# A vision tower's feed-forward on tokens sorted by expert, and softplus split into Exp, Ln and a clip

## The chip, the cores and the metric

The kernel runs on one core of one Trainium2 chip. Five engines work in parallel, each with its own queue of instructions: PE (TensorE, matmuls and transpositions), DVE (VectorE), ACT (ScalarE, functions from tables), POOL (GpSimd) and SP, which here only issues DMAs. They wait for each other by semaphores. The metric is the device time of one launch in microseconds; a run's time is a little longer than the span that the profile shows.

## The reference

All in float32. x is (4, 512, 256, 4), the stream h is 4 batches of 512 tokens of width 256.

```python
h = einsum('bhid,oi,od->bho', x, weighted_sum, weight)
h = h + attn(layernorm(h))        # 4 layers, the same weights in each:
    # x = rmsnorm(x) ; xr = x @ W_in ; x_in, res = split(xr)
    # u = silu(conv4(x_in) + conv_b) ; dbl = u @ W_x  -> dt, B, C
    # delta = softplus(dt @ W_dt + b_dt)
    # h_t = exp(delta_t * A) * h_(t-1) + delta_t * u_t * B_t   (16 states, 512 channels)
    # y = sum_state(h_t * C_t) + u * Dp ; x = (y * silu(res)) @ W_out
h = h + ffn(layernorm(h)):
    # z = layernorm(h)
    # e = argmax(z @ W_router)                  (4 experts, one for each token)
    # t = gelu(z @ W1[e] + b1[e])               (256 -> 1024)
    # out = layernorm(t @ Wo + bo + z) * gamma + beta
```

## The kernel before, in words

The program has three parts. It begins with the token product and its norm. Then comes the scan stage: 16 steps k, one batch of one layer each (k = layer * 4 + batch). A step walks over 16 states s and, in each, over four quarters d of the 512 channels; one pair (s, d) is a slot. In a slot TensorE transposes delta\*u\*B into one of two PSUM banks (`b_states`) and transposes a finished state back, adding it to y (`sum_states`, two states later), VectorE runs the scan along the 512 tokens, ScalarE makes the decays exp(delta\*A) and most products with B, and GpSimd multiplies the scanned state by C, two quarters at a time.

Everything else of the layer is strewn into the slots by tables written out by hand (`X_AT`, `WDT_AT`, `TAP_AT`, `GATING_AT` and others): step k + 1's projections, convolution taps and softplus, step k + 2's norm, step k - 1's output projection. Each engine goes through its own loop over (k, s, d) in this order, so an instruction that waits holds up all behind it on its engine. Softplus is one ScalarE instruction for each quarter (`softplus`, L519), with b_dt as its bias, out of the PSUM bank into which `to_delta` put the product; the bank is used again two quarters later, so `to_delta(k, d)` waits for delta of quarter d - 2.

The feed-forward works batch by batch on tokens that lie along the free axis. The router's choice becomes four masks of 0 and 1 spread over the partitions (`rows`, `mask`), VectorE multiplies z by each, and TensorE adds up the products of all four masked copies with the four W1 in one PSUM bank:

```python
nc.tensor.matmul(work_ps[c % 4], b1_sb[:, c * P:(c + 1) * P], f_rows[b], start=True, stop=False)
for e in range(EXPERTS):
    for m in range(DC):
        last = nc.tensor.matmul(work_ps[c % 4], w1_sb[e][:, 2 * m + rows // SEQ, rows % SEQ:rows % SEQ + P],
                                zm(b, e)[:, m, :], start=False, stop=e == EXPERTS - 1 and m == DC - 1)
```

All four W1 and Wo are loaded once, in the last step (`load_w1`, `load_wo`). The head of batch 0 (norm, router, masks) lies in the last step's slots, that of batch b + 1 among the dense products of batch b (`dense`), and the tail's norm of batch b - 1 as well.

## Time and profile before

| | |
|---|---|
| median of 3 runs | 2142.24 us (2139.98 to 2143.46) |
| profiled execution | 2141.26 us, of it span 2139.5 us |
| PE busy | 2021.1 us (94%) |
| DVE busy | 1500.3 us (70%) |
| ACT busy | 1448.3 us (68%) |
| POOL busy | 1483.4 us (69%) |
| mean of all DMA | 53 GB/s |

Busy shares are means over stages with different limits, and a busy PE is not PE at its peak. In the tables of the profile a line is that of the kernel's text; "idle before" is the idle time of the engine just before these instructions, with what ended it.

### The profile page before, as it was taken

How to read it: one execution, taken by the hardware profiler on the slowest of the kernel's cores; microseconds unless marked ns; L12 is line 12 of the kernel's file. 1: busy time of each engine (PE TensorE's matmuls, PEld its weight loads, DVE VectorE, ACT ScalarE, POOL GpSimd, SP SyncE). 2: the span in 40 equal slices, each digit the busy share in tenths (PEclk: the TensorE clock that was granted, in tenths of full speed). 3: DMA queues.
4: the chain of work that ended last, by engine and by line, in shares of the span. 5: the costliest groups of instructions: out<-in, count | busy, mean ns of one | idle time of the engine just before them, and what ended most of it. 6: DMA issues, size and time to landing. Idle time of an engine off the chain costs nothing.

```text
span 2139.5 us, 30859 instructions
## 1 busy us (share of the span) xinstructions
PE 2021.1 (94%) x11952; PEld 1440.0 (67%) x11952; DVE 1500.3 (70%) x1509; ACT 1448.3 (68%) x2294; POOL 1483.4 (69%) x845
## 2 busy tenths in 40 slices
PE   6989899999999999999999999999998889999997
PEld 3457677777777777877777777777777754444443
DVE  1368988889898989898988889898988860120101
ACT  0268898888989888988898988988898721000000
POOL 0039898989898998989898989898989940000000
PEclk9989999999999999999999999999999999999999
DMA  5211112111111111111112111211112410000000
GB/s 186 90 60 41 50 42 70 42 61 46 65 40 61 46 62 63 42 68 41 61 42 70 42 61 41 69 41 61 40 51 82 145 59 11 0 30 0 10 0 20
DMA packets 34137, 113.13 MB, mean 53 GB/s; under 512 B 6148, under 2 KB 8836, under 8 KB 33480
## 3 DMA queue, kind: packets, MB, share of 16 engines
q1 hardware_dynamic: 33992, 111.17, 15.3%
q8 instruction: 95, 1.56, 0.3%
q14 instruction: 50, 0.41, 0.1%
HBM read 95.95 MB, written 15.20 MB: 52 GB/s over the span
## 4 chain that ended last, share of the span: by engine, by line
PE 45%; POOL 18%; DVE 13%; issue 11%; ACT 11%; DMA 1%; SPq 0%; DVEq 0%; POOLq 0%; ACTq 0%
POOL hid L419 13%; PE b_ps L1110 8%; DVE hid L858 8%; PE y_all L1121 6%; ACT dub_t L559 5%; ACT hid L546 5%; PE y_all L1219 5%; PE b_ps L1219 5%; POOL dub_t L410 4%; DVE u L733 3%; PE y_all L922 3%; PE bank_b L1003 2%; PE y_all L1128 2%; PE y_all L1232 2%; PE bank_b L1018 2%
## 5 line engine op out<-in xcount | busy, mean ns | idle before, releaser
L858 DVE TENSOR_TENSOR_SCAN hid<-hid,b_ps 128x512 f32<-128x512 f32 x1024 | 1213.8, 1211 | 200.0 <-PE b_ps L1110 178.7
L419 POOL TENSOR_TENSOR hid<-hid,c_rep 128x1024 f32<-128x1024 f32 x512 | 1209.8, 2395 | 159.6 <-DVE hid L858 159.3
L1110 PEld LDWEIGHTS b_ps<-ident,dub_t 128*128 128x128 f32 x4096 | 485.6, 143 | 367.8 <-issue 218.3
L1110 PE MATMUL b_ps<-ident,dub_t 128*128 128x128 f32 x4096 | 631.5, 277 | 61.2 <-DVE hid L858 56.1
L546 ACT ACTIVATE hid<-delta,neg_a 128x512 f32<-128x512 f32 x1024 | 652.9, 711 | 0.4
L1121 PE MATMUL y_all<-ident,hid 128*128 128x128 f32 x4096 | 617.9, 274 | 19.7 <-POOL hid L419 19.6
L559 ACT ACTIVATE dub_t<-du_t,b_t 128x512 f32<-128x512 f32 x768 | 490.3, 712 | 57.8 <-PE b_ps L1110 56.1
L1121 PEld LDWEIGHTS y_all<-ident,hid 128*128 128x128 f32 x4096 | 481.2, 142 | 26.1 <-POOL hid L419 26.1
L410 POOL TENSOR_SCALAR dub_t<-du_t,b_t 128x512 f32<-128x512 f32 x256 | 173.8, 714 | 0.0
L733 DVE SCALAR_TENSOR_TENSOR u<-bank_b,conv_w_sb,u 128x511 f32<-128x511 f32 (+2 forms) x192 | 139.7, 728 | 0.7
L1003 PE MATMUL bank_b<-xn,w_in_sb 128*128 128x512 f32 x256 | 134.0, 611 | 3.3 <-DVE u L733 3.3
L584 ACT ACTIVATE hid<-b_ps 128x512 f32<-128x512 f32 x16 | 9.5, 596 | 175.8 <-PE b_ps L1219 108.4
L424 POOL TENSOR_TENSOR f_norm<-f_norm,half_power 128x4 f32<-128x4 f32 x4 | 4.1, 1016 | 173.9 <-DVE f_norm L773 173.9
L1095 PE MATMUL bank_a<-y_d,w_out_sb 128*128 128x512 f32 x240 | 123.6, 597 | 0.0
L428 POOL TENSOR_TENSOR f_norm<-f_norm,half_power 128x4 f32<-128x4 f32 x4 | 4.0, 1006 | 169.9 <-DVE f_norm L828 169.9
L584 ACT ACTIVATE hid<-y_all 128x512 f32<-128x512 f32 x16 | 9.6, 597 | 127.0 <-PE y_all L1219 127.0
L400 POOL TENSOR_TENSOR du<-delta,u 128x1024 f32<-128x1024 f32 x32 | 76.5, 2392 | 6.4 <-ACT delta L519 6.4
L524 ACT ACTIVATE du_t<-bank_a 128x512 f32<-128x512 f32 x64 | 37.9, 592 | 59.1 <-PE bank_a L1063 59.1
L922 PE MATMUL y_all<-hid,dub_t 128*128 128x512 f32 x128 | 62.6, 632 | 15.5 <-DMA hid<-x_t 15.5
L1018 PE MATMUL bank_b<-w_in_sb,xn 128*128 128x512 f32 x128 | 67.2, 609 | 1.1 <-DVE u L733 1.1
L1128 PE MATMUL y_all<-diag_skip,u 128*128 128x128 f32 x512 | 67.6, 275 | 0.0
L1018 PE MATMUL bank_a<-w_in_sb,xn 128*128 128x512 f32 x128 | 66.7, 605 | 0.1
(192 smaller groups left out, 1770.5 us busy)
## 6 DMA issues: line engine op xcount, KB each, us to landing
c_rep<-bc_dram SPq DMA_DIRECT2D x128, 512.0 KB, 3.7
hid<-x_t SPq DMA_DIRECT2D x4, 2048.0 KB, 8.9
x_dram<-x_out SPq DMA_DIRECT2D x16, 512.0 KB, 2.8
xt<-x_dram SPq DMA_DIRECT2D x15, 512.0 KB, 3.6
h_dram<-hid SPq DMA_DIRECT2D x4, 512.0 KB, 3.3
out<-y_d SPq DMA_DIRECT2D x4, 512.0 KB, 2.6
x_dram<-hid SPq DMA_DIRECT2D x3, 512.0 KB, 2.7
c_rep<-x_dram SPq DMA_DIRECT2D x3, 512.0 KB, 5.9
```

What stands on the lines that cost most here:

```text
L410: nc.gpsimd.tensor_scalar(dub_t[:, i % DUB, tc, :], du_t[:, k % 2, tc, :], b_t[:, k % 2, tc, s:s + 1], 1.0, ALU.mult, ALU.mult).then_inc(d ...
L419: nc.gpsimd.tensor_tensor(part, part, c_rep[:, n % 2, s % GROUP, :].unsqueeze(1) .broadcast_to([P, HALF, SEQ]), ALU.mult).then_inc(hc_read ...
L546: nc.scalar.activation(hid[:, i % RING, d, :], delta[:, k % 2, d, :], ACT.Exp, scale=neg_a[:, d, s:s + 1]).then_inc(decay_ready, 1)
L559: nc.scalar.activation(dub_t[:, i % DUB, tc, :], du_t[:, k % 2, tc, :], ACT.Copy, scale=b_t[:, k % 2, tc, s:s + 1]).then_inc(dub_act, 1)
L733: nc.vector.scalar_tensor_tensor(u[:, k % 2, m, t:], bank_b[:, 0:SEQ - t], conv_w_sb[:, m, w:w + 1], u[:, k % 2, m, t:], ALU.mult, ALU.add ...
L858: nc.vector.tensor_tensor_scan(hid[:, i % RING, d, :], hid[:, i % RING, d, :], b_ps[d % 2][:, :], 0.0, ALU.mult, ALU.add)\
L922: last = nc.tensor.matmul(y_all[:, DC * (b % 2) + m, :], wc[:, kc, m * P:(m + 1) * P], hid[:, 2 * (b % 2) + kc // NI, kc % NI, :], start=k ...
L1003: ins = nc.tensor.matmul(bank_b[:, :], w_in_sb[:, c, m * P:(m + 1) * P], xn[:, c, :], start=c == 0, stop=c == DC - 1)
L1018: ins = nc.tensor.matmul((bank_a if tc % 2 == 0 else bank_b)[:, :], xn[:, c, tc * P:(tc + 1) * P], w_in_sb[:, c, INNER:], start=c == 0, st ...
L1110: last = nc.tensor.transpose(b_ps[d % 2][:, c * P:(c + 1) * P], dub_t[:, i % DUB, c, d * P:(d + 1) * P], ident[:, :])
L1121: last = nc.tensor.matmul(y_ps[d][:, c * P:(c + 1) * P], hid[:, i % RING, d, c * P:(c + 1) * P], ident[:, :], start=s == 0 and c == 0, sto ...
L1219: last = nc.tensor.matmul(work_ps[c % 4], w1_sb[e][:, 2 * m + rows // SEQ, rows % SEQ:rows % SEQ + P], zm(b, e)[:, m, :], start=False, sto ...
```

## The change

Two things are changed. **Softplus**: b_dt becomes a row of the product (a row of ones in `dbl`, the bias in `w_dt_sb`), ScalarE computes Exp and then Ln(1 + .), and VectorE takes min(that, max(x, 60)). One table set is loaded by hand behind the last gate, since it holds both functions. GpSimd's products u\*delta move behind one more of its products with C.

**Feed-forward**: h is turned so that tokens lie on the partitions, and norms become BN_STATS and BN_AGGR. For each pair of batches (1024 tokens) the chosen experts are counted by matmuls with a triangle and with ones (`rank`), which gives each token a row in a list sorted by expert, each expert's part rounded up to whole tiles of 128 rows: at most 8 + 3 = 11 tiles a pair, 22 in all (`lay_out`). GpSimd scatters z's rows there in DRAM (`send_z`), SP reads them back as tiles, and for each tile GpSimd gathers the W1 of its expert, 1 MB, into one of five buffers (`load_w1`). A tile is one product with one W1 (`expert`), a gelu with the picked bias, and a projection (`project_out`); its rows go to DRAM (`store_y`) and are gathered back in the order of tokens (`fetch_y`) for the last norm. Both lists in DRAM are filled with zeros at the start.

```diff
 GROUP = 2
+TILES = CH + EXPERTS - 1
+ALL_TILES = 2 * TILES
+WBUF = 5
...
                     load_tok(0)
                     load_tok(1)
+                    sp.wait_ge(zero_made, 1)
+                    for g in range(2):
+                        sp.dma_start(z_dram[g].rearrange("(j p) o -> p j o", p=P),
+                                     du[:, 0, 0:D].unsqueeze(1).broadcast_to([P, TILES, D])).then_inc(z_zeroed, 16)
                     sp.dma_start(w_in_sb[:, :, :], w_in.rearrange("(c p) n -> p c n", p=P)).then_inc(weights_in, 16)
...
                         if k == STEPS - 1:
-                            load_hx(0)
+                            load_x_tokens(0)
+                            load_h(1)
+                            load_x_tokens(1)
...
-                                if live(k + 1) and (s, half) == (6, 0):
+                                if live(k + 1) and (s, half) == (6, 1):
                                     times_u(k + 1, 0)
-                                if live(k + 1) and (s, half) == (7, 0):
+                                if live(k + 1) and (s, half) == (7, 1):
                                     times_u(k + 1, 1)
...
+                    def load_w1(t):
+                        g, j, q = t // TILES, t % TILES, t % WBUF
+                        pool.wait_ge(rows_ready, g + 1)
...
+                        if t >= WBUF:
+                            pool.wait_ge(work_done, 2 * (t - WBUF + 1))
+                        nc.gpsimd.indirect_dma_start(out=w1_buf[q], out_offset=None, in_=w1,
+                                                     in_offset=bass.IndirectOffsetOnAxis(ap=w_row[:, g, j:j + 1], axis=0))\
+                            .then_inc(w1_in[q], 16)
+
+                    def send_z(g):
...
+                        for c in range(CH):
+                            nc.gpsimd.indirect_dma_start(out=z_dram[g], out_offset=bass.IndirectOffsetOnAxis(ap=pos[:, g, c:c + 1], axis=0),
+                                                         in_=f_z[PAIR * g + c // TC][:, c % TC, :], in_offset=None).then_inc(z_out[g], 16)
...
+                        for c in range(TC):
+                            i = (b % PAIR) * TC + c
+                            nc.gpsimd.indirect_dma_start(out=y_tok[b][:, c, :], out_offset=None, in_=y_dram[g],
+                                                         in_offset=bass.IndirectOffsetOnAxis(ap=pos[:, g, i:i + 1], axis=0))\
+                                .then_inc(y_back[b], 16)
...
-                    def softplus(k, d):
+                    def delta_exp(k, d):
                         act.wait_ge(wdt_done, NI * k + d + 1)
-                        nc.scalar.activation(delta[:, k % 2, d, :], (bank_a if d % 2 == 0 else bank_b)[:, :], ACT.Softplus,
-                                             bias=vec_sb[:, 1, d:d + 1]).then_inc(delta_ready, 1)
+                        nc.scalar.activation(delta[:, k % 2, d, :], (bank_a if d % 2 == 0 else bank_b)[:, :], ACT.Exp)\
+                            .then_inc(exp_ready, 1)
+
+                    def delta_log(k, d):
+                        act.wait_ge(exp_ready, NI * k + d + 1)
+                        nc.scalar.activation(delta[:, k % 2, d, :], delta[:, k % 2, d, :], ACT.Ln, bias=1.0).then_inc(log_ready, 1)
...
                                 gate(k + 1, 3)
+                                nc.scalar.preload_act_table_set("natural_log_exp_and_others")
...
+                    def softplus(k, d):
+                        dve.wait_ge(log_ready, NI * k + d + 1)
+                        nc.vector.scalar_tensor_tensor(delta[:, k % 2, d, :], (bank_a if d % 2 == 0 else bank_b)[:, :], 60.0,
+                                                       delta[:, k % 2, d, :], ALU.max, ALU.min).then_inc(delta_ready, 1)
...
+                    SOFTPLUS_AT = {(7, 0): 0, (7, 1): 1, (8, 0): 2, (8, 1): 3}
...
-                                if live(k + 2) and at == (8, 2):
-                                    normalize(k + 2)
...
+                                if live(k + 2) and at == (8, 3):
+                                    normalize(k + 2)
...
+                    def expert(t):
...
+                        for c in range(FC):
+                            for m in range(DC):
+                                last = nc.tensor.matmul(work_ps[t % 2][c // NI][:, (c % NI) * P:(c % NI + 1) * P],
+                                                        w1_buf[q][:, m * FF + c * P:m * FF + (c + 1) * P], z_tile[t // 2 % 2][:, t % 2, m, :],
+                                                        start=m == 0, stop=m == DC - 1, skip_group_check=True)
...
+                    H_TURN_AT = {(0, 2): (0, 0), (1, 2): (0, 1), (8, 2): (1, 0), (9, 2): (1, 1)}
+                    Z_TURN_AT = {(5, 3): (0, 0), (6, 3): (0, 1), (12, 2): (1, 0), (13, 1): (1, 1)}
+                    LOGITS_AT = {(7, 2): 0, (14, 0): 1}
...
-                                if live(k + 2) and at == (8, 1):
+                                if live(k + 2) and at == (8, 2):
                                     spread_norm(k + 2)
```

On VectorE, the order in the middle of a step, from the mean square of the norm in slot (6, 0) to the first convolution tap, before; L858 is the scan:

```order
L713 TENSOR_SCALAR norm<-bank_a 128x4
L858 SCALAR_TENSOR_TENSOR hid<-hid,b_ps 128x512
L738 COPY b_t<-bank_b 128x64
L858 SCALAR_TENSOR_TENSOR hid<-hid,b_ps 128x512 x9
L720 TENSOR_TENSOR xn<-xt,bank_b 128x1024
L858 SCALAR_TENSOR_TENSOR hid<-hid,b_ps 128x512 x4
L728 TENSOR_SCALAR u<-bank_b,conv_w_sb,vec_sb 128x512
```

The same place of the changed kernel, where L1043 is the scan and L838 the normalisation:

```order
L861 COPY b_t<-bank_b 128x64
L1043 SCALAR_TENSOR_TENSOR hid<-hid,b_ps 128x512 x3
L856 SCALAR_TENSOR_TENSOR delta<-bank_a,delta 128x512
L1043 SCALAR_TENSOR_TENSOR hid<-hid,b_ps 128x512
L856 SCALAR_TENSOR_TENSOR delta<-bank_b,delta 128x512
L1043 SCALAR_TENSOR_TENSOR hid<-hid,b_ps 128x512 x3
L856 SCALAR_TENSOR_TENSOR delta<-bank_a,delta 128x512
L1043 SCALAR_TENSOR_TENSOR hid<-hid,b_ps 128x512
L856 SCALAR_TENSOR_TENSOR delta<-bank_b,delta 128x512
L1043 SCALAR_TENSOR_TENSOR hid<-hid,b_ps 128x512 x2
L838 TENSOR_TENSOR xn<-xt,bank_b 128x1024
L1043 SCALAR_TENSOR_TENSOR hid<-hid,b_ps 128x512 x3
```

Four clips (L856) now stand among the scans, and the normalisation has moved one slot on, behind the tenth scan instead of the ninth.

On TensorE, in the feed-forward, a dense chunk of one batch and its projection before (u, delta, du and du_t hold the four W1, gate_t holds Wo):

```order
L1216 MATMUL y_all<-w_dt_sb,b_sb 128x512
L1219 MATMUL y_all<-dub_t,u 128x512 x2
L1219 MATMUL y_all<-dub_t,delta 128x512 x2
L1219 MATMUL y_all<-dub_t,du 128x512 x2
L1219 MATMUL y_all<-dub_t,du_t 128x512 x2
L1232 MATMUL y_all<-hid,gate_t 128x512 x16
```

Two tiles of the changed kernel (L1418 transposes the sorted rows, L1434 is the expert's product, L1449 the projection of the tile before; delta and du_t are buffers of gathered W1, dub_t holds Wo):

```order
L1418 MATMUL bank_b<-ident,hid 128x128 x4
L1434 MATMUL y_all<-hid,du_t 128x128 x16
L1449 MATMUL bank_a<-dub_t,hid 128x256 x8
L1434 MATMUL b_ps<-hid,delta 128x128 x16
L1449 MATMUL bank_a<-dub_t,hid 128x256 x8
```

A chunk used to be nine products of 512 columns, 32 times, and a tile is now 16 of 128 and 8 of 256 columns, 22 times.

On GpSimd, behind the last product with C, the DMAs that it issues for the first pair and the start of the second:

```order
L530 DMA delta<-L_ffn_W,w_row 128x2048
L539 DMA z_dram<-du,pos 1408x256 x8
L530 DMA du_t<-L_ffn_W,w_row 128x2048
L530 DMA gate_t<-L_ffn_W,w_row 128x2048
L530 DMA delta<-L_ffn_W,w_row 128x2048
L530 DMA du_t<-L_ffn_W,w_row 128x2048
L509 TENSOR_TENSOR f_norm<-f_norm,half_power 128x4 x2
L530 DMA delta<-L_ffn_W,w_row 128x2048
L530 DMA du_t<-L_ffn_W,w_row 128x2048
L530 DMA gate_t<-L_ffn_W,w_row 128x2048
L539 DMA z_dram<-hid,pos 1408x256 x8
```

GpSimd issued no DMA before; all in this queue is new but the roots (L509). Behind the rows shown come the gathers of W1 for tiles 8 to 21 and, in two blocks of eight, those of y.

## Rows read from the trace of the kernel before

**Rows 1.** Windows: length, busy us of PE, PEld, DVE, ACT, POOL; clock, DMA share, GB/s.
```profile
81.00:1590.00 1509.00, 1445.22 (x9748) 1121.50 (x9747) 1289.22 (x1272) 1295.61 (x2056) 1323.05 (x740) 0.99 0.16 53
1590.00:1747.00 157.00, 134.86 (x1006) 113.94 (x1004) 134.74 (x123) 112.17 (x181) 142.51 (x79) 0.97 0.25 85
...
1893.00:1960.00 67.00, 67.00 (x168) 29.36 (x168) 11.44 (x14) 4.39 (x7) 2.37 (x3) 0.97 0.07 24
```

**Rows 2.** Timeline of TensorE: start, length, group, count.
```profile
958.58 1.06 PE L1128 MATMUL y_all<-diag_skip,u 128*128 128x128 f32 x8
...
2109.31 13.90 PE L1232 MATMUL y_all<-hid,gate_t 128*128 128x512 f32 x32
```

**Rows 3.** Line L738: duration ns min/median/max, first and last start.
```profile
L738 DVE COPY b_t<-bank_b x16: 198/200/224, 101.7 to 1587.5; 128x64 f32<-128x64 f32 x16
```

**Rows 4.** Timelines of VectorE and TensorE in the middle of step 8.
```profile
988.38 3.44 DVE L858 TENSOR_TENSOR_SCAN hid<-hid,b_ps 128x512 f32<-128x512 f32 x3 [0.51 <-PE b_ps L1110]
...
993.88 4.71 DVE L858 TENSOR_TENSOR_SCAN hid<-hid,b_ps 128x512 f32<-128x512 f32 x4 [0.51 <-PE b_ps L1110]
998.51 1.19 DVE L720 TENSOR_TENSOR xn<-xt,bank_b 128x1024 f32<-128x1024 f32 x1
...
1003.39 1.22 DVE L858 TENSOR_TENSOR_SCAN hid<-hid,b_ps 128x512 f32<-128x512 f32 x1 [0.33 <-PE b_ps L1110]
...
992.31 1.02 PE L1051 MATMUL bank_b<-dbl,w_dt_sb 128*128 128x512 f32 x2
...
999.84 1.05 PE L1003 MATMUL bank_b<-xn,w_in_sb 128*128 128x512 f32 x2
```

**Rows 5.** Groups by form: busy us, mean ns of one, idle before.
```profile
L419 POOL TENSOR_TENSOR hid<-hid,c_rep 128x1024 f32<-128x1024 f32 x512 | 1209.8, 2395 | 159.6 <-DVE hid L858 159.3
L733 DVE SCALAR_TENSOR_TENSOR u<-bank_b,conv_w_sb,u 128x511 f32<-128x511 f32 x64 | 46.7, 729 | 0.3
L502 ACT ACTIVATE u<-u 128x512 f32<-128x512 f32 x64 | 35.0, 630 | 0.0
L519 ACT ACTIVATE delta<-bank_a,vec_sb 128x512 f32<-128x512 f32 x32 | 21.9, 683 | 6.7 <-PE bank_a L1051 6.5
L519 ACT ACT_TABLE_LOAD x16 | 20.5, 1283 | 0.3
L393 POOL TENSOR_TENSOR norm<-norm,half_power 128x4 f32<-128x4 f32 x16 | 16.7, 1041 | 34.8 <-DVE norm L713 34.8
```

**Rows 6.** DMA issues: count, KB each, median us from issue to landing.
```profile
hid<-x_t SPq DMA_DIRECT2D x4, 2048.0 KB, 8.9
out<-y_d SPq DMA_DIRECT2D x4, 512.0 KB, 2.6
w_in_sb<-L_attn_W_in SPq DMA_DIRECT2D x1, 1024.0 KB, 14.3
du_t<-L_ffn_W SPq DMA_DIRECT2D x1, 1024.0 KB, 7.7
xn<-x_dram SPq DMA_DIRECT2D x1, 512.0 KB, 4.5
```

**Rows 7.** Timelines of SP's queue and TensorE at the last step's start.
```profile
1649.52 0.43 SPq L293 DMA_DIRECT2D c_rep<-bc_dram  x1
...
1645.03 0.60 PE L1110 MATMUL b_ps<-ident,dub_t 128*128 128x128 f32 x4
```

**Rows 8.** Timelines: VectorE instructions with two inputs in SBUF.
```profile
1669.28 3.44 DVE L762 TENSOR_TENSOR xt<-xt,xn 128x1024 f32<-128x1024 f32 x1
...
1711.65 4.95 DVE L787 TENSOR_TENSOR top<-logit 128x8 f32<-128x8 f32 x1
...
1831.83 1.22 DVE L762 TENSOR_TENSOR hid<-hid,c_rep 128x1024 f32<-128x1024 f32 x1
```

**Rows 9.** Timeline of VectorE: the last scans, and the first work behind the last projection.
```profile
1743.54 2.32 DVE L858 TENSOR_TENSOR_SCAN hid<-hid,b_ps 128x512 f32<-128x512 f32 x2
...
2123.25 1.41 DVE L818 SCALAR_TENSOR_TENSOR y_d<-y_all,fvec,xn 128x512 f32<-128x512 f32 x2 [35.41 <-PE y_all L1232]
```

More of the change, by code:

```diff
@@ new lines, in build @@
+            y_tok = [tokens(c_rep[:, q, :, :]) for q in range(2)] + \
+                    [yg_t[:, DC * q:DC * q + DC, :, :].rearrange("p a b c -> p (a b c)").rearrange("p (c o) -> p c o", o=D)
+                     for q in range(2)]
+            w1_buf = [t.rearrange("p a b -> p (a b)") for t in
+                      (delta[:, 0, :, :], du_t[:, 0, :, :], gate_t[:, 0, :, :], delta[:, 1, :, :], du_t[:, 1, :, :])]
+            wo_sb = dub_t[:, 1, :, :]
+            work_ps = [[b_ps[0][:, :], b_ps[1][:, :]], [y_ps[0], y_ps[1]]]
@@ new lines, in fetch_y @@
+                    def fetch_y(b):
+                        g = b // PAIR
+                        for q in range(2):
+                            pool.wait_ge(y_stored[q], 32 * (3 if g == 0 else (TILES + 1 - q) // 2))
+                        for c in range(TC):
[3 more added lines that the diff above has]
+                                .then_inc(y_back[b], 16)
@@ L1341, in _ @@
                     out_x(last - 1, 1, 3)
[L1342 to L1350 removed]
+                    for dc in range(NI):
+                        last_back(dc)
+                    h_turn(2, 0)
+                    h_turn(2, 1)
                     last_out(0)
[L1352 removed]
@@ L1395, in _ @@
-                    project_out(BATCH - 1)
-                    tail_mean(BATCH - 1)
-                    tail_var(BATCH - 1)
-                    tail_spread(BATCH - 1)
+                    tile_turn(0)
+                    expert(0)
+                    for t in range(ALL_TILES):
+                        if t % 2 == 0 and t + 2 < ALL_TILES:
+                            tile_turn(t // 2 + 1)
+                        if t + 1 < ALL_TILES:
+                            expert(t + 1)
+                        if t in (0, 2):
+                            z_turn(2 + t // 2, 0)
+                            z_turn(2 + t // 2, 1)
+                        if t in (1, 3):
+                            logits(2 + t // 2)
+                        if t == 4:
+                            rank(1)
+                        project_out(t)
```

917 lines of the change are left out of this document (506 added, 411 removed).

## The prediction

> **What bounds the kernel now.** I read the windows first, then the page's groups, then stretches of the timeline. The windows split the span in two programs [rows 1]. From 81 to 1747 us runs the scan stage: TensorE, VectorE and GpSimd are all near 90% busy, the sign of engines that hand work to each other slot by slot. From 1747 us to the end runs the feed-forward, and there TensorE alone is busy: 67.00 of 67.00 us in the middle windows, with VectorE near 10 us. So every microsecond of TensorE work removed behind 1747 us counts in full until something else takes over.
>
> The output projection is 16 fp32 matmuls of 128x512; the trace counts 32, so each is issued as two passes, and 32 passes take 13.90 us, 0.43 us a pass [rows 2]. One chunk of the dense layer is 1 bias and 8 products, 18 passes, 7.8 us; there are 32 chunks: 250 us. The projection comes four times: 55 us. With masks, norms and the last step's own projection the feed-forward lasts 393 us, from the last scan's end at 1745.9 [rows 9] to 2139.5.
>
> In the scan stage a step (one batch of one layer) takes (1587.5 - 101.7)/15 = 99.05 us [rows 3]. Which engine sets it changes inside a step. The VectorE timeline [rows 4] shows scans at a pitch of 1.13 us where nothing is between them (988.38, three in 3.44), and idle times of 0.33 to 0.51 us behind TensorE where that also does projections. Behind the last row begin the convolution's taps, one between two scans, and there VectorE hardly idles.
>
> **Part 1: softplus.** Removed: 64 ScalarE softplus (0.68 us) and 31 table loads, since one set now serves Exp and Ln: two loads per step instead of four [rows 5]. Added on ScalarE: 64 Exp and 64 Ln, priced by the silu row, 0.63. Per step: out 4 x 0.68 + 2 x 1.28 = 5.3 us, in 8 x 0.63 = 5.0 us. I count it as nothing: ScalarE's decays run about a state ahead of the scans that use them; were that cover gone, it would be worth 0.3 us a step. The Trainium skill (ScalarE: Activation LUTs, Table sets) budgets about 2.7 us for a table load and names the joint set of exp and ln; by it 31 loads would be worth 84 us instead of the row's 40 us, if they were on the path.
>
> Added on VectorE: 64 clips, PSUM and SBUF in, SBUF out. The tap row is the same form: 0.73 us, and its share beside a scan about 0.65 [rows 5]. Four per step, 2.6 us. Where do they fall? Behind the scans of slots (7,0), (7,1), (8,0), (8,1), where VectorE idled up to 0.51 us behind TensorE. I walk the stretch from 988.38, where three scans stand, (6,3), (7,0) and (7,1). Scan (7,0) ends at 990.6 and clip 0 behind it at 991.3; scan (7,1) and clip 1 end at 993.1. TensorE's product 2 waits for clip 0, product 3 for clip 1 (they reuse the PSUM bank): product 3 moves from 992.3 to 993.05, so the next scan from 993.88 to 994.55. Scan (8,0) runs at 995.7, clip 2 ends at 997.4, clip 3 at 999.2. The spreading of the norm waits for clip 3; the normalisation, 998.51 before, starts at 1001.5; TensorE's first input product waits for it until 1002.65 (999.84 before), with the scans' transposes queued behind it. Scan (9,2) starts at 1005.9 instead of 1003.39: **+2.5 us per step**. Nothing gives it back: behind it VectorE is saturated. GpSimd, whose products u x delta each move behind one more of its other products, comes late by only 0.7 us by the same walk, less than VectorE does. 14 steps at 2.5, one without a normalisation at 1.6, one ahead of the pipeline at 1: **+38 us**. Bounds: 0, if it is all absorbed, and 16 x 2.6 plus the two handshakes of 0.7 us each, 64 us. I take the walk.
>
> **Part 2: the start.** Two stores of zeros (2.9 MB) go ahead of the weights on SP's queue. The 1 MB W_in, issued at 7.2, needed 14.3 us behind 4 MB of x [rows 6]; 2.9 MB more at that queue's rate is 10 to 14 us. The squares that TensorE waits for come near 46 us, the weights then at 35 to 39. I take +1 us, range 0 to 6.
>
> **Part 3: the last step.** Its router work for two batches lies among the scans, as that of one batch did. New: a transposition of h in slot (0,2) that waits for the tokens of x. On SP's queue this load stands right behind the load of C issued at 1649.52 [rows 7]; with 4.5 us to landing [rows 6] that is 1654.5. TensorE starts the slot at 1645.03 and would reach the transposition near 1646: 8 us of stall, with the scan's transposes behind it. Part comes back, because GpSimd limits this step (142.51 busy of 157.00 [rows 1]). Against it, two VectorE instructions with both inputs in SBUF waited here: 3.44 us where the same sum takes 1.22 later, and 4.95 us for a 128x8 [rows 8]. Before had both; after has two choices and eight 128x256 scalings. **+4 us**, from -6 to +29 (six such groups at 4.8 us). The Trainium skill (SBUF — State Buffer, Who interferes with whom) says a VectorE instruction with two SBUF inputs, or in a two-port mode, and a GpSimd one exclude each other for a whole instruction. By that rule the eight scalings block too; the two rows agree with it for two inputs, and no row shows scalings.
>
> **Part 4: the feed-forward.** PE per tile of 128 tokens, from the pitch of 128-column passes: eight diagonal passes take 1.06 us, 0.17 of it the last one's tail, 0.111 us each [rows 2]. 32 passes: 3.56 us. The projection, 16 passes of 256 columns at half of 0.43: 3.44 us. Two transposes 0.22. Sum 7.2 us; 22 tiles: 159 us instead of 305. Router remains of two batches, ranks, logits: 7 us, handovers 4. **170 us.**
>
> Ahead of it, from the last scan's end: layout arithmetic 3 us; then one gather and eight scatters issued by GpSimd. No row shows one. Bounds for one issue: 0.43 us, SP's issue of a plain DMA [rows 7], and 2.4 us, GpSimd's big product; I take 1.2, near its smallest instruction, 1.04 [rows 5], since 128 offsets are little data. 9 x 1.2 = 10.8 us, landing 2.2 (2.6 for 512 KB [rows 6]), reading z back 4.5, transposing and copying 1.5, two more for sharing with five W1 tiles: **24 us**. The other chain, last output projection, its store, reload and join, gives about the same.
>
> Feeding: 1 MB of W1 per tile. The same 1 MB took 7.7 us alone, 2 MB of x 8.9 us [rows 6], so queued tiles stream at about 4.5 us, below 7.5: hidden, but the eight scatters of the second pair hold up gather 8: 3 us.
>
> Behind the last projection: copy 0.6, store 2.9, eight gathers of 1.2 with 2 us landing, then VectorE's norm of two batches in series, each one sum of 128x1024 (1.2 us, as the normalisation [rows 4]) and nine small ones, 3.4, then four scalings and two such passes, 3.8; the root on GpSimd behind the gathers, store 2.9: **30 us** (16 now, from 2123.25 [rows 9]).
>
> **Sum.** 1745.9 + 1 + 38 + 4 = 1788.9; + 24 + 170 + 3 + 30 = 2015.9 of span. The profiled execution is 1.8 us longer than its span and 1.0 under the median of the runs: **2018 us**.
>
> **Rivals.**
> - Gathers bound: at 7.7 us a MB plus 0.4 MB of rows of z and y per tile, 9.2 us instead of 7.5: 22 x 1.7 = +37, 2055 us. For it: that row. Against: it is a lone load. TensorE would wait on W1 at every tile.
> - Issue on GpSimd dear: at 2.4 us, 13 at the start and 8 at the end add 25 us: 2043 us. The Trainium skill (DMA: Bandwidth & Descriptors, Anatomy of one DMA) gives about 2.0 us fixed plus bytes over 436 GB/s for a GpSimd DMA; an estimate by it is 4.4 us per W1 tile, which would leave the sum as it is.
> - The port rule: all six groups of two-input and scaling instructions in the last step block for 4.8 us: 29 us instead of 4, 2043 us. For it: [rows 8]. Against: before paid two of these waits too, and GpSimd's queue runs dry sooner when VectorE stands. It is the Trainium skill's rule named in part 3.
> - The clips are hidden: -38, 1980 us. For it: VectorE does idle in the stretch [rows 4]. Against: the walk.
> - Slower: a gather of scattered rows as slow as W_in's 14.3 us per MB [rows 6]. 22 x 14.3 = 315 us instead of 173: 2160 us. It decides from 13.5 us a tile on, where 22 tiles take 173 + 124 us and the gain is gone. For it: no indirect DMA is in any row. Against: each row is 8 KB in one piece, and W_in's time was mostly queueing.
>
> **How the numbers follow.** Forecast 0.52, gathers bound 0.13, dear issue 0.09, port rule 0.07, clips hidden 0.12, slower 0.06, no change 0.01. The range, 1980 to 2060, takes in the bounds of parts 1, 3 and 4 short of the slow gather. 0.2% (4 us) is about what a measurement here tells from no change: faster 0.93, within it 0.01, slower 0.06.
>
> **What would show it.** The step's pitch between copies of b_t: 101.5 us. In the tile windows TensorE near 95% busy, pitch 7.5 us, no wait on W1 but near tile 8. The last scan near 1789 us, the first tile 24 us later, 30 us behind the last projection. Wrong it would be if the step's pitch stays at 99 or passes 104, or if TensorE waits for W1 in every tile.

## The result, and the profile after

The changed kernel took 2063.05 us (median of 4 runs, 2061.11 to 2073.18), the kernel before 2142.85 us (4 runs): ratio 0.9633, 95% interval 0.9603 to 0.9664. The forecast was 2018 us with a range of 1980 to 2060. The direction was right and the gain came where the prediction saw it, but some 45 us of it are missing: the time lies just above the upper end of the range.

The profiled execution is the longest of the four, 2073.18 us with a span of 2071.5, so what is measured against this trace below looks up to 10 us better than it is. The windows of it, cut where its stages end (columns as in [rows 1]):

```profile
81.00:1650.00 1569.00, 1453.13 (x9752) 1126.43 (x9751) 1324.14 (x1330) 1285.00 (x2083) 1325.12 (x739) 0.99 0.15 52
1650.00:1834.00 184.00, 144.63 (x1054) 130.46 (x1053) 144.15 (x158) 114.44 (x189) 144.21 (x80) 0.91 0.18 61
1834.00:1864.00 30.00, 17.59 (x98) 14.74 (x95) 12.22 (x38) 3.96 (x7) 16.32 (x15) 0.89 0.74 268
1864.00:2041.00 177.00, 172.44 (x1164) 162.09 (x1165) 45.68 (x110) 53.33 (x181) 37.92 (x36) 0.96 0.41 147
2041.00:2071.00 30.00, 0.73 (x4) 0.30 (x2) 14.64 (x33) 0.00 (x0) 9.92 (x10) 0.57 0.23 79
```

The five stretches are the scan stage up to the last copy of b_t (in the middle of step 14), the rest of the scan stage (the end of step 14 and the whole of step 15, called the last stretch from here on), the way to the first tile, the tiles, and what stands behind the last projection. From the last scan's end to the end the kernel now takes 237 us instead of 393. TensorE is still busy 172.44 of 177.00 us among the tiles. But the last stretch has become slack: in [rows 1] TensorE was busy 86% of it, here 79%, and GpSimd 78% instead of 91%. TensorE's granted clock there was 0.91 instead of 0.97.

The copies of b_t, line L861 now, answer to [rows 3]:

```profile
L861 DVE COPY b_t<-bank_b x16: 198/200/225, 102.7 to 1649.6; 128x64 f32<-128x64 f32 x16
```

The step's pitch is (1649.6 - 102.7)/15 = 103.1 us, 4.1 more than before; the prediction had 2.5 and named 104 as the limit of being right. From the last copy to the end of the last scan it is 184.5 us (1834.1 - 1649.6), before 158.4 (1745.9 - 1587.5).

The middle of a step, for VectorE and then TensorE, answers to [rows 4]:

```profile
1032.49 0.67 DVE L856 SCALAR_TENSOR_TENSOR delta<-bank_a,delta 128x512 f32<-128x512 f32 x1
...
1026.84 1.13 PE L1247 MATMUL bank_a<-dbl,w_dt_sb 128*128 128x512 f32 x2 [0.60 <-DVE delta L856]
...
1033.21 0.66 PE L1281 MATMUL bank_a<-ident,yg_t 128*128 128x128 f32 x4 [1.76 <-DVE delta L856]
...
1036.36 0.62 PE L1189 MATMUL bank_b<-ident,norm 128*128 128x128 f32 x4 [0.74 <-DVE delta L856]
```

A clip takes 0.67 us, as priced. The walk in the prediction knew the first wait (product 2 for clip 0) and the third (the norm's spreading for clip 3). It did not have the second and longest, which 13 of the steps have: L1281 turns the gated outputs into the bank that clip 2 still reads, in slot (8,0), ahead of the spreading. In the list of TensorE's waits in the stretch from 81 to 1650 us (who waits, for whom, us in total, times, longest):

```profile
PE bank_a L1281 <- DVE delta L856: 22.9, 13, 1.8
```

### The profile page after: what moved, and what is told of

The parts are those of the page before. It is cut to its first block, busy times and chain, and to the rows that moved or that the text cites. A ratio compares the mean times of both kernels' runs of the same rounds, so it can differ in the third digit from the quotient of the medians.

```text
span 2071.5 us, 31985 instructions
## 1 busy us (share of the span) xinstructions
PE 1850.7 (89%) x12240; PEld 1465.2 (71%) x12240; DVE 1564.5 (76%) x1703; ACT 1464.7 (71%) x2467; POOL 1538.3 (74%) x896
## 4 chain that ended last, share of the span: by engine, by line
PE 52%; DVE 19%; issue 12%; ACT 12%; POOL 2%; DMA 2%; SPq 0%; DVEq 0%; POOLq 0%; ACTq 0%
PE b_ps L1316 12%; DVE hid L1043 10%; PE y_all L1327 9%; ACT dub_t L694 6%; ACT hid L681 5%; DVE u L851 4%; PE bank_b L1199 3%; PE bank_a L1449 3%; PE y_all L1118 3%; PE bank_b L1214 3%; PE bank_a L1223 3%; PE b_ps L1434 2%; PE y_all L1434 2%; PE bank_a L1247 2%; PE bank_a L1214 2%
## 5 line engine op out<-in xcount | busy, mean ns | idle before, releaser
L1043 DVE TENSOR_TENSOR_SCAN hid<-hid,b_ps 128x512 f32<-128x512 f32 x1024 | 1218.3, 1210 | 243.2 <-PE b_ps L1316 222.8
L1296 PE MATMUL bank_a<-y_d,w_out_sb 128*128 128x512 f32 x192 | 98.3, 594 | 0.0
L992 DVE COPY hid<-bank_a 128x512 f32<-128x512 f32 x11 | 7.6, 692 | 95.6 <-PE bank_a L1449 95.6
L1449 PE MATMUL bank_a<-dub_t,hid 128*128 128x256 f32 x352 | 79.7, 380 | 0.0
L1449 PEld LDWEIGHTS bank_a<-dub_t,hid 128*128 128x128 f32 x352 | 65.3, 190 | 8.0
L669 ACT ACTIVATE x_out<-bank_a 128x512 f32<-128x512 f32 x30 | 17.7, 589 | 73.6 <-PE bank_a L1296 46.1
```

Of the source, the lines that this page charges most:

```text
L1043: nc.vector.tensor_tensor_scan(hid[:, i % RING, d, :], hid[:, i % RING, d, :], b_ps[d % 2][:, :], 0.0, ALU.mult, ALU.add)\
L1449: last = nc.tensor.matmul(bank_a[:, (t % 2) * D:(t % 2 + 1) * D], inter[t % 2][:, c, :], wo_sb[:, c // 2, (c % 2) * D:(c % 2 + 1) * D], st ...
```

## The experiments

All runs are listed here. "Pitch" is that of the b_t copies over 15 steps, "last" the last stretch, from the last copy to the end of the last scan. Every kernel's trace, that of before too, has some steps in which the granted clock of TensorE falls from its upper level (2.4 GHz) to its lower (1.2 GHz) for some 3.4 us around the copy of b_t. "Falls" counts them at the 14 copies from the second to the fifteenth, and "clean step" is the pitch that most steps without a fall have. All four come from the one profiled execution of each run, and the number of falls need not be the same in its other executions. combo_old_slots has eight more falls at other places of its steps, and its clean step is that of steps without these too.

| run | median us | ratio to before, 95% | pitch | clean step | falls | last |
|---|---|---|---|---|---|---|
| the kernel before | 2142.9 | 1 | 99.1 | 100.2 | 4 | 158.4 |
| the changed kernel | 2063.1 | 0.9633 (0.9603-0.9664) | 103.1 | 104.4 | 5 | 184.5 |
| one_pass | 2007.2 | 0.9376 (0.9361-0.9392) | 98.7 | 100.2 | 1 | 184.8 |
| one_pass_slots | 2030.7 | 0.9487 (0.9472-0.9501) | 100.6 | none; 102.4 with | 14 | 181.4 |
| no_clip | 2033.1 | 0.9466 (0.9431-0.9502) | 100.8 | none; 102.4 with | 14 | 185.1 |
| no_clip_alt | 2031.8 | 0.9479 (0.9464-0.9493) | 100.8 | none; 102.4 with | 14 | 185.2 |
| no_clip_slots | 2008.7 | 0.9377 (0.9362-0.9393) | 99.2 | 100.3 | 5 | 184.5 |
| clip_short | 2046.2 | 0.9552 (0.9536-0.9568) | 101.8 | 103.0 | 4 | 179.8 |
| back_slot | 2053.9 | 0.9591 (0.9568-0.9613) | 102.0 | 103.1 | 5 | 185.6 |
| clip_early | 2049.2 | 0.9557 (0.9531-0.9582) | 102.2 | 103.3 | 6 | 181.7 |
| before_new_softplus | 2204.3 | 1.0294 (1.0277-1.0311) | 103.2 | 104.4 | 5 | 160.7 |
| turn_later | 2052.2 | 0.9571 (0.9549-0.9592) | 102.8 | 104.4 | 3 | 174.8 |
| act_scale | 2051.6 | 0.9582 (0.9565-0.9599) | 102.9 | 104.4 | 3 | 174.9 |
| z_first | 2059.7 | 0.9620 (0.9603-0.9637) | 103.2 | 104.4 | 4 | 180.8 |
| combo | 2033.6 | 0.9498 (0.9485-0.9511) | 102.4 | 103.3 | 6 | 166.1 |
| combo_back | 2029.1 | 0.9483 (0.9464-0.9502) | 101.8 | 103.1 | 5 | 167.0 |
| combo_slots | 2026.0 | 0.9464 (0.9448-0.9480) | 101.5 | 102.8 | 4 | 166.5 |
| combo_norm_slots | 2018.6 | 0.9425 (0.9407-0.9443) | 100.6 | 102.2 | 2 | 167.0 |
| combo_old_slots | 2047.9 | 0.9563 (0.9542-0.9583) | 103.0 | 103.2 | 5 | 171.0 |

What a fall costs can be read where one stands alone. In one_pass the two steps beside its only one took 100.6 and 101.3 us instead of 100.2, which is 1.5 us more. The last stretch scatters by itself: ten kernels whose last step is the changed kernel's own have from 179.8 to 185.6 us.

### Which half of the change moved what

**before_new_softplus**: the kernel before with the new softplus (its functions as in the diff above, with the clips, the bias row and the moved slots), and the old feed-forward.

> The kernel before with the new softplus alone: Exp, Ln, clip, the bias as a row of the product, the moved slots, and the old feed-forward. Theory A (the two halves of the change add): pitch 103.1, time 2143 + 62 = 2205 us. Rival D (the growth needs the new feed-forward's loads and layout, or the walk's 2.5 us was right for this part): pitch 101.5, time 2181 us or less.

2204.3 us, 61 more than before; pitch 103.2, and the last stretch only 2.3 us longer. Theory A holds to a microsecond. So the new softplus costs 61 us with the old feed-forward as well, and of the 26 us by which the last stretch grew all but some 2 belong to the new feed-forward.

**one_pass**: the changed kernel with the old shape of the softplus: one ScalarE pass, of another function, so that delta has other values, no clip, the old slots, and no table set loaded by hand.

```
-    act.wait_ge(wdt_done, ...); activation(delta, bank, ACT.Exp).then_inc(exp_ready, 1)
-    act.wait_ge(exp_ready, ...); activation(delta, delta, ACT.Ln, bias=1.0).then_inc(log_ready, 1)
+    act.wait_ge(wdt_done, ...); activation(delta, bank, ACT.Sigmoid).then_inc(delta_ready, 1)
-    softplus(k + 1, SOFTPLUS_AT[at])        # the clip on VectorE
-    spreading (8, 2), normalisation (8, 3), u x delta (6, 1), (7, 1)
+    spreading (8, 1), normalisation (8, 2), u x delta (6, 0), (7, 0)
```

> The changed kernel with the delta made as before in one ScalarE pass that signals delta itself, no Ln, no clip, four table loads a step, and the normalisation, its spreading and GpSimd's products u x delta back in their old slots. The pass is a Sigmoid in place of the softplus, so the values of delta are not the reference's. Theory A (all of the step's growth of 4.1 us is the new softplus): the pitch between copies of b_t falls from 103.1 to 99.1 us and the time from 2063 to 2002 us. Rival B (part of the pitch comes from something else in the change, such as the bias row or code placed differently): pitch 100 to 102, time 2015 to 2045.

2007.2 us, 56 less than the changed kernel, and a clean step of 100.2 us as before: the whole growth of the step is the softplus part. Its last stretch is still 184.8 us.

### What inside the softplus part costs the 4 us a step

**no_clip**: only the clip is gone.

```
-    activation(delta, delta, ACT.Ln, bias=1.0).then_inc(log_ready, 1)
+    activation(delta, delta, ACT.Ln, bias=1.0).then_inc(delta_ready, 1)
-    softplus(k + 1, SOFTPLUS_AT[at])
```

> The changed kernel without the four VectorE clips of a step: Ln writes delta and signals it. The clip, which acts only where the projection passes 60, is left out. Theory A (the clips' 2.6 us of VectorE and the TensorE wait for clip 2 make the growth): pitch 99.1, time 2002 us. Rival B (it is the chain Exp, Ln on ScalarE that makes delta late, whoever clips): the pitch stays above 101.5 and the time above 2038 us.

2033.1 us, pitch 100.8: between the two, and so a miss for both. By the pitches the clips are worth 2.4 us a step, and 2.1 remain. But the trace has something beside it: at all 14 copies of b_t the clock falls, where the changed kernel's trace has five falls, so the two pitches don't differ by the clips alone. A step takes 102.4 us with its fall. Less 1.5 us for the fall, an estimate from one_pass's steps, that is 100.9 us, and against 104.4 the clips with their waits are worth 3.5 us a step, not 2.4.

**clip_short**: all four clips stay with all their waits, on 64 columns.

```
-    scalar_tensor_tensor(delta[:, k % 2, d, :], bank[:, :], 60.0, delta[:, k % 2, d, :], ALU.max, ALU.min)
+    scalar_tensor_tensor(delta[:, k % 2, d, 0:64], bank[:, 0:64], 60.0, delta[:, k % 2, d, 0:64], ALU.max, ALU.min)
```

> The changed kernel with each clip of 64 columns instead of 512 (the other 448 are left unclipped): all waits stay, VectorE's time for them falls from 0.67 to about 0.2 us. Theory A (most of the step's growth is the clips' own time on VectorE, the rest the wait for clip 2): 4 x 0.47 = 1.9 us a step less, 28 us in all, 2035 us. Rival B (the growth is the chain of waits TensorE, ScalarE, VectorE, TensorE, in which the clip's length counts only where it is last, for clips 2 and 3): 15 x 0.9, 2049 us or more.

2046.2 us, pitch 101.8. A clip takes 0.20 us in the groups of its trace:

```profile
L856 DVE SCALAR_TENSOR_TENSOR delta<-bank_a,delta 128x64 f32<-128x64 f32 x32 | 6.4, 200 | 4.2 <-ACT delta L655 4.2
```

That is 1.9 us of VectorE taken out of a step for 1.4 us won (104.4 to 103.0), and the time is nearer to rival B. So it isn't mainly VectorE's occupation: of the 3.5 us estimated above, 2.1 remain when the clips are nearly empty. TensorE still waits 16.9 us for clip 2 ahead of L1281, 13 times, instead of 22.9.

**back_slot**: `BACK_AT = {..., (8, 0): 2, (8, 3): 3}` becomes `{..., (8, 1): 2, (8, 3): 3}`.

> The changed kernel with one number changed: the transposition of the gated outputs, third group, stands in slot (8,1) instead of (8,0), so that TensorE waits for clip 2 behind one more transposition for the scans. Theory A (that wait of 1.76 us a step is what the walk in the prediction left out, 4.1 against 2.5 us): pitch about 101.5, time 2040 us. Rival C (the wait only takes the place of the one for clip 3 behind it): pitch 103.1, time 2063 us.

2053.9 us, pitch 102.0, and a clean step of 103.1 instead of 104.4: between A's 1.6 and C's nothing. The wait of L1281 for the clip is smaller, not gone: 7.8 us in all instead of 22.9, still 13 times. It does not pass on to the spreading, as C had it, since the spreading's wait for clip 3 falls too, from 11.0 to 4.8 us.

**clip_early**: ScalarE's order (the same for clips 0 and 1) and one slot.

```
-    delta_exp(k + 1, 2); delta_exp(k + 1, 3); delta_log(k + 1, 2); delta_log(k + 1, 3)
+    delta_exp(k + 1, 2); delta_log(k + 1, 2); delta_exp(k + 1, 3); delta_log(k + 1, 3)
-    SOFTPLUS_AT = {(7, 0): 0, (7, 1): 1, (8, 0): 2, (8, 1): 3}
+    SOFTPLUS_AT = {(7, 0): 0, (7, 1): 1, (7, 3): 2, (8, 1): 3}
```

> The changed kernel with ScalarE's order Exp, Ln, Exp, Ln instead of Exp, Exp, Ln, Ln, and VectorE's clip 2 in slot (7,3) instead of (8,0). Theory A (1.8 us of each step is TensorE's wait for clip 2, whose Ln stands behind the next product's Exp): the wait at the third transposition group goes, pitch in the middle steps 103 instead of 104.4, time 2040 us. Rival B (VectorE's clips set the pitch wherever they stand): 2063 us.

2049.2 us, pitch 102.2, clean step 103.3: less than A said, and clearly not B. L1281 waits 8.5 us in all instead of 22.9. Order and slot were moved together, so no run tells which of the two did it. back_slot and this run work on the same wait from its two ends: combo_back, which has both, has no wait of that line left and a clean step of 103.1, no better than back_slot's. That one wait is worth 1.3 us a step.

**no_clip_alt**: no_clip with clip_early's order on ScalarE.

> The run without clips once more, with ScalarE's order Exp, Ln, Exp, Ln. The clip is left out. Without clips in the old order TensorE's granted clock fell to 1.2 GHz for some 3.7 us in every step, which alone lengthened the stretch by 1.7 us. Theory A (the clip explains the growth, the clock dip hid the rest of it): if the dip is gone, the pitch in the middle steps is 100.3 us and the time 2063 - 62 - 1 = 2000 to 2008 us. Rival B (Exp and Ln in two passes cost 2 us a step by themselves): pitch 102.4, time 2033 us, with the clock at full speed.

2031.8 us, pitch 100.8: as no_clip, with the clock falling in each step again (for 3.4 us by the trace; the 3.7 in what was expected is too long). It told nothing apart, because the fall came with it. Two cross runs did.

**one_pass_slots**: one_pass with the changed kernel's slots, that is spreading (8,2), normalisation (8,3), u x delta (6,1), (7,1). **no_clip_slots**: no_clip with the old ones.

> The run with one ScalarE pass (a Sigmoid in place of the softplus, so delta has other values), but with the changed kernel's slots: normalisation in (8,3) instead of (8,2), its spreading in (8,2) instead of (8,1), the products u x delta half a slot group later. Theory A (the later normalisation makes TensorE's first input product wait 0.75 us each step): 15 x 0.75, 2007 + 11 = 2018 us, pitch of middle steps 101.0. Rival B (the slots are free, the rest is the passes' or the clock's): 2007 us, pitch 100.2.

> Exp and Ln in two passes, no clip (it is left out), and the old slots for the normalisation, its spreading and u x delta. Theory A (slots 0.75 us, clock dip 1.45 us, passes nothing): no wait for the normalised x; pitch 101.7 if the dip stays, 100.2 and 2007 us if it goes. Rival B (the two passes cost 2 us a step by themselves): pitch 102.4 and 2033 us.

2030.7 and 2008.7 us. With one pass and the new slots the kernel is as slow as with two passes and no clip; with two passes and the old slots it is as fast as with one. So the two passes cost nothing that matters (1.5 us in all, as the prediction said), and the moved slots cost 24 us in both pairs, neither of which has a clip. Waits show part of it: TensorE's first input product (L1188) waits for the normalised x 14 times, 10.8 us in all, with the new slots, and not at all with the old ones. The wait as one_pass_slots's trace lists it (waiting engine and line, the awaited, us in total, times, longest):

```profile
PE bank_b L1188 <- DVE xn L829: 10.8, 14, 1.1
```

Nearly all of the rest is the clock. Here is one_pass_slots at its b_t copy (1000.0), windows of 4 us, columns as before:

```profile
996.00:1000.00 4.00, 4.00 (x28) 3.75 (x28) 2.41 (x3) 4.00 (x7) 4.00 (x2) 0.77 0.00 0
1000.00:1004.00 4.00, 4.00 (x21) 2.59 (x20) 1.65 (x4) 3.47 (x6) 3.80 (x3) 0.81 0.36 131
```

and one_pass at the same place, its copy at 982.1:

```profile
978.00:982.00 4.00, 4.00 (x33) 3.47 (x33) 2.40 (x4) 4.00 (x8) 4.00 (x3) 1.00 0.00 0
982.00:986.00 4.00, 3.93 (x30) 3.16 (x29) 3.09 (x5) 3.97 (x6) 4.00 (x3) 1.00 0.34 131
```

TensorE is busy 4.00 of 4.00 us in both ahead of the copy, with the same work (16 products of one column for the norm, 1.84 us, transposes of the scans, 8 products of 16 columns for b_t); in the first the clock drops from its upper level to the lower in part of each window, and the step loses 1.4 us (102.4 us from copy to copy instead of 100.2 to 100.3, less the wait of 0.77). In one_pass_slots this happens at all 14 copies, in one_pass at one of them (880.8 us), in no_clip_slots at five.

This does not carry over to the changed kernel. It has the new slots too, and its trace has five falls, the kernel before's four. So the falls explain next to nothing of its 61 us, and what the later normalisation costs it is the wait.

### What lengthened the last step

These rows of the changed kernel show it, of TensorE, then SP, then VectorE:

```profile
1718.17 1.12 PE L1366 MATMUL bank_b<-ident,xt 128*128 128x128 f32 x4 [9.62 <-DMA w_in_sb<-x_dram]
...
1751.02 0.66 PE L1316 MATMUL b_ps<-ident,dub_t 128*128 128x128 f32 x4 [4.39 <-DVE hid L1043]
...
1711.62 0.32 SPq L357 DMA_DIRECT2D x_dram<-x_out  x1
1711.98 0.43 SPq L351 DMA_DIRECT2D c_rep<-bc_dram  x1
1712.46 0.79 SPq L374 DMA_DIRECT2D w_in_sb<-x_dram  x1
...
1745.33 4.51 DVE L906 TENSOR_SCALAR du<-w_in_sb,moments,f_norm 128x256 f32<-128x256 f32 x4
...
1797.93 4.56 DVE L906 TENSOR_SCALAR du<-w_in_sb,moments,f_norm 128x256 f32<-128x256 f32 x4
...
1856.29 1.38 DVE L906 TENSOR_SCALAR hid<-u,moments,f_norm 128x256 f32<-128x256 f32 x4 [1.16 <-POOL f_norm L509]
```

TensorE stands 9.6 us for the tokens of x. Their load (L374) is issued behind the load of C (L351), as the prediction had it, and that stands behind the store of x (L357), for which SP's queue waits 11.1 us until ScalarE has copied it; the tokens land 5.7 us after the issue. And four scalings take 4.5 us twice while GpSimd multiplies, 1.4 us where it doesn't; TensorE stands 4.4 us behind them. The second group takes 4.5 us in every run that has it. The first took 2.4 to 2.5 us in z_first, clip_early, clip_short and one_pass_slots, whose last stretches are the shortest of those with an untouched last step.

**turn_later**:

```
-    H_TURN_AT = {(0, 2): (0, 0), (1, 2): (0, 1), ...}   JOIN_AT = {(1, 0): (0, 0), (2, 1): (0, 1), ...}
+    H_TURN_AT = {(1, 2): (0, 0), (2, 2): (0, 1), ...}   JOIN_AT = {(2, 0): (0, 0), (3, 1): (0, 1), ...}
-    MOMENTS_AT (2, 3), head_root (3, 0), SCALE_AT (4, 2), Z_TURN_AT (5, 3), Z_T_COPY_AT 6
+    MOMENTS_AT (3, 3), head_root (4, 0), SCALE_AT (5, 1), Z_TURN_AT (6, 1), Z_T_COPY_AT 7
```

> The changed kernel with the first two transpositions of h in the last step moved from slots (0,2), (1,2) to (1,2), (2,2), their joins, moments, root, scaling and the first transposition of z two to four slots later with them. Theory A (the last step is 26 us longer than before, 9.6 of them TensorE's wait at 1708 us for the tokens of x, which land 6.9 us later than the slots in between would have taken): wait 2.7 us, time 2056 us. Rival B (the step is bound by GpSimd and gives such a wait back): the wait goes, the time stays within 2 us of 2063.

2052.2 us; the last stretch is 9.7 us shorter. The wait itself is not gone, but it is 5.46 us instead of 9.62:

```profile
1714.57 1.12 PE L1366 MATMUL bank_b<-ident,xt 128*128 128x128 f32 x4 [5.46 <-DMA w_in_sb<-x_dram]
```

More was won than the wait's 4.2 us. The later scalings are not the rest, since they still take 3.95 and 4.54 us. TensorE's wait for ScalarE at L1394 is shorter by 2.9 us (0.7 instead of 3.6), and what then remains lies within the scatter of this stretch.

**act_scale**:

```
-    for c in range(TC): tensor_scalar(f_z, f_h2, moments, f_norm, ALU.subtract, ALU.mult).then_inc(z_ready, 1)
+    scalar_tensor_tensor(shift, moments, -1.0, f_norm, ALU.mult, ALU.mult).then_inc(shift_ready, 1)      # VectorE
+    for c in range(TC): activation(f_z, f_h2, ACT.Identity, bias=shift, scale=f_norm).then_inc(z_ready, 1)  # ScalarE
```

> The changed kernel with the eight 128x256 scalings of the last step done by ScalarE (scale and shift per partition) instead of VectorE; VectorE forms the shift in one 128x4 instruction. Theory A (four scalings take 4.5 us on VectorE while GpSimd multiplies, 1.4 us otherwise, twice, and TensorE and GpSimd stand behind them): 2 x 4.2 us less, time 2055 us. Rival B (the wait for GpSimd passes on to the next VectorE instruction with two inputs in SBUF, or the step hides them): 2063 us.

2051.6 us; the last stretch is 9.6 us shorter, A's 8.4 within the scatter. On ScalarE one scaling takes 589 ns, behind VectorE's shift.

**z_first**: `head_root(2)` goes ahead of the W1 gathers 1 to 4 on GpSimd, and between them stands `pool.wait_ge(z_in[0][0], 16)`.

> The changed kernel with GpSimd's W1 gathers 1 to 4 held until the first 512 KB of sorted z have landed. Theory A (those 4 MB share the queues with the read of z, which took 13.0 us instead of some 4, and with the store of x): first tile 7 us earlier, time 2056 us. Rival B (what is won there is lost to the second tile's W1, which then comes late): 2063 us, with a wait for W1 of about 6 us at the second tile.

2059.7 us, 3.4 less, not 7. The read of z now lands in 3.7 us instead of 13.0, and TensorE has no wait for W1 at the second tile. But the first tile stands 26.5 us behind the last scan, and kernels with the old order of gathers have 26.4 to 30.5 there: a gain of 1 to 3 us, not settled. TensorE's last output projection now ends just ahead of the first tile, so the other chain (store and reload of x), for which TensorE waits 7.4 us there, is the one that binds. The prediction had said that both give about the same.

### Together

**combo** is clip_early, turn_later, act_scale and z_first in one, with the shift and the scalings of the first group in slots that suit both moves ((4,3) and state 6); **combo_back** adds back_slot; **combo_slots** puts clip 3 in (8,0) as well; the last two set slots of the softplus part back.

> The four moves that each gained, together in the changed kernel: clips early, turning of h later, scalings on ScalarE, z read ahead of the W1 gathers; nothing is left out. Theory A (they lie in different places, the last step's two in different halves of it): 2063 - 14 - 11 - 11.5 - 3.5 = 2023 us. Rival B (the last step is bound by GpSimd once one of its two stalls is gone, and the second gives nothing): 2034 us.

> The combination with the third group's transposition in slot (8,1) as well. Theory A (clip 2 comes early there, the wait is gone already): no change against the combination, within 3 us. Rival B (the wait for clip 2 is still last by some 0.5 us a step): 8 us faster than the combination.

> The combination with the third group's transposition in (8,1), and clip 3 one slot earlier, in (8,0); nothing is left out. Theory A (TensorE's spreading still waits 0.7 us for clip 3 in each step, and the first input product 1.1 us behind it): 0.7 us a step, 10 us, 2019 us. Rival B (VectorE's time is what counts there, wherever clip 3 stands): 2029 us.

> The combination with clips 2 and 3 in slots (7,3) and (8,0), and all the slots that the change had moved set back: spreading in (8,1), normalisation in (8,2), the products u x delta half a group earlier. Nothing is left out. Theory A (the slots have a cost of their own, 0.75 us of waiting for the normalised x and the clock dips): at least 0.9 us a step less, 2026 - 14 = 2012 us. Rival B (they were the clips' price: TensorE's spreading now waits for clip 3 and GpSimd's product for clip 1): 2026 us or more.

> The same with only the spreading and the normalisation set back, u x delta in its new slots. Theory A (it is the wait for the normalised x): the same time as with all set back, within 3 us. Rival C (GpSimd's products u x delta make the difference): 2026 us, as the combination with its new slots.

combo: 2033.6 us, which is rival B's number but not its reason: the last stretch fell by 18.4 us, the sum of the two moves (9.7 + 9.6). The four medians had summed to 40 us; in the traces, clip_early's steps are 12.3 us shorter up to the last copy (combo's 10.8), the last stretches 9.7 and 9.6 and the way to the first tile 3.5 at most (combo's 2.8). That is 32 us found again in combo's trace, and 29.5 in its median. The traces differ by 40 all the same, because the tiles took 169.4 us in combo's and 177.6 in the changed kernel's longest execution, with no move among them. The sum of 40 had such scatter in it, put down to the moves. combo_back is 4.5 us faster, half of B's 8, combo_slots another 3, both inside what their runs scatter.

combo_norm_slots, with only the spreading and the normalisation back in (8,1) and (8,2), takes 2018.6 us: ratio 0.9425 to before, and 0.9425/0.9633 = 0.978 of the changed kernel. Setting u x delta back as well costs 29 us, 2047.9: GpSimd's product then waits for the clip 16 times, 56.5 us in all instead of 16.1, with the products by C queued behind it:

```profile
POOL du L487 <- DVE delta L868: 56.5, 16, 4.7
```

So the theory was half right. The normalisation's later slot was a cost of its own that the clips don't need: against combo_slots, which differs in nothing else, 7.4 us in the medians and 0.6 us in the clean step (102.8 to 102.2). The later slot of u x delta is the clips' price and worth paying. combo_norm_slots leaves nothing out and is the fastest of all versions that compute the whole softplus.

## Why the prediction came out as it did

**The feed-forward** (part 4) held in its mechanism and came 10 us too long. Span from the last scan's end: 24 + 173 + 30 = 227 us were forecast, 237.4 came. The tiles lasted 177.6 us in this profile at a mean granted clock of 0.96, and 169.3 to 178.2 us in the profiles of the other kernels with the same tiles, the shortest ones at 1.00. The forecast of 173 lies within that. The issue of an indirect DMA on GpSimd, taken at 1.2 us, shows here:

```profile
1839.13 1.02 POOL L539 DMA_INDIRECT z_dram<-du,pos  x1 [0.31 <-issue]
1840.46 0.98 POOL L539 DMA_INDIRECT z_dram<-du,pos  x1 [0.30 <-issue]
```

1.0 us, one every 1.3 us. Of the gathers' stall at the second pair 3 us were forecast; TensorE stood 3.3 us between 1928 and 1936 us, where the DMA engines were busy throughout (share 0.98); the trace names no releaser there, so that it was the gather is likely and not shown. Elsewhere it did not stand for W1: rival "gathers bound" is out, "dear issue" and "slower" too. Behind the last projection 30 us were forecast and 29.8 came:

```profile
2041.77 0.69 DVE L992 COPY hid<-bank_a 128x512 f32<-128x512 f32 x1 [9.79 <-PE bank_a L1449]
```

The first tile came 30 us behind the last scan, not 24. The read of z took 13.0 us where I had given two extra for sharing with W1; in z_first, with that read at 3.7 us, the way was 26.5 us, so up to 3.5 of the 6 were that.

**The start** (+1 us) held: the first copy of b_t went from 101.7 to 102.7.

**First failed step: the walk through the middle of the step (part 1), +2.5 us a step and 38 us in all; 4.1 and 61 came.** The prices of the instructions were right; the waits were not. A clean step grew from 100.2 to 104.4 us. The walk left out that the third group of transpositions (L1281) reuses the bank that clip 2 still reads, with Ln 2 late behind the next product's Exp. Moving the transposition (back_slot) returns 1.3 us a step, moving the Ln and the clip (clip_early) 1.1, both together 1.3: one wait, and most of the 1.7 us that the walk lacked (4.2 against 2.5). And it took the normalisation's later slot for a consequence of clip 3, while it is an edit with a cost of its own: 0.77 us of waiting a step without clips, 0.6 us a step given back in combo_norm_slots.

In a staircase of runs, each with one thing more: one_pass 2007, with the new slots 2031, with two passes 2033, with the clips 2063. These differences are not prices of the things in the changed kernel: the falls of the clock go from 1 to 14 at the second stair and from 14 back to 5 at the last, so the second looks dearer and the last cheaper than it is.

**Second failed step: the last step (part 3), +4 us; 26.1 came.** The stall on the tokens of x was forecast at 8 us and was 9.6, in the queue order that the prediction read from [rows 7]. What failed is what followed: "part comes back", because GpSimd limited this step. It did not come back. GpSimd's share of it fell from 91 to 78%, and turn_later and act_scale each returned some 10 us, 18.4 together. How much each returned is uncertain by some 5 us, the scatter of this stretch. The rival "port rule" had the mechanism with too high a price: six groups at 4.8 us. Two groups of scalings came at 4.5 us, 3.1 too many each, and stand on the path with what follows them; the other groups were small. With both moves the last stretch is still 8 us longer than before (166.1 against 158.4), and those 8 stay open. So does the part of the clock: the mean granted clock of the last stretch was 0.97 before, 0.91 in the changed kernel and 0.95 in combo, and no run tells what the stalls cost by themselves from what they cost by a lower clock behind them.

Both failed terms lie inside bounds that the prediction gave them, 0 to 64 us and -6 to +29, near their upper ends. The two ends together would have put the time at 2069 us; the stated range stopped at 2060.

The Trainium skill (SBUF — State Buffer, Who interferes with whom) has this rule: a VectorE instruction in a two-port mode and a GpSimd one lock each other out. The rows above agree with it also for scalings with one tensor input and two scalars per partition, 4.5 us beside GpSimd's products and 1.4 without; the last step of before had none of 128x256. Nothing in the sums above rests on it.

With the measured terms the sum closes: 2015.9 + 23 (loop) + 22 (last step) + 6 (first tile) + 5 (tiles) = 2072, and the profile's span is 2071.5. The other runs are some 10 us shorter, with a mean granted clock of 0.976 instead of 0.971.

## What to carry to other kernels

When an engine is given a new step between two others, list every later reader and writer of the buffer it holds, not only its two neighbours in the dependence chain: the costly wait was that of a third party which reuses the bank. Price a moved slot by itself, apart from what it was moved for; here one of two moved slots had to stay and the other was worth more set back. When two runs differ in more than the edit (here in how often the clock fell), compare steps in which that did not happen. And a stall in a step "with slack elsewhere" should be counted in full unless a row shows what would make it up.

## What the hardware showed that I had not expected

- The granted clock of TensorE can fall at the same place of a loop step, the copy of b_t, while TensorE is busy without a break ahead of it: 4.00 of 4.00 us in the window of one_pass_slots that holds the start of a fall. Every kernel's trace here has such falls. Their number goes with where neighbouring instructions stand: in the profiled executions 14 of 14 in the three runs with the new slots and no clips, 1 and 5 with the old slots and no clips, 3 to 6 in the kernels with clips and the new slots. One alone cost 1.5 us. The kernels with the changed feed-forward also scatter more, up to 16 us (no_clip: 2018.8 us at a mean granted clock of 0.971, 2034.8 at 0.964), where the kernel before stayed between 2136.5 and 2145.7 us over all its runs. What triggers a fall the runs don't tell.
- An indirect DMA of 128 rows costs GpSimd 1.3 us from one to the next, about half of one of its big products (2.4 us). A plain 512 KB read beside four 1 MB gathers took 13.0 us, with the gathers held back 3.7.
